# A transformer layer in fp32 with 16 experts on one Trainium2 core: attention and projection joined in one stage, row-maxima pieces, list matmuls and last loads in another order

## The reference

```python
def _L0_attn_ref(x, W_qkv, W_proj):          # 2048 tokens, D = 512, 16 heads of 32
    qkv = x @ W_qkv.T
    attn = jnp.einsum('bhqd,bhkd->bhqk', q, k) * SCALE
    attn = jnp.where(causal[None, None], attn, -jnp.inf)
    out = jnp.einsum('bhqk,bhkd->bhqd', jax.nn.softmax(attn, axis=-1), v)
    return out.transpose(0, 2, 1, 3).reshape(b, s, d) @ W_proj.T
def _moe_forward(x, gate_w, w_gate, w_up, w_down):       # E = 16, K = 6
    scores = jax.nn.softmax(h @ gate_w.T, axis=-1)
    topk_w, topk_idx = jax.lax.top_k(scores, K)
    cw = jnp.zeros((T, E)).at[jnp.arange(T)[:, None], topk_idx].add(topk_w)
    for e in range(E):
        y = y + cw[:, e:e + 1] * (silu(h @ w_gate[e].T) * (h @ w_up[e].T) @ w_down[e].T)
x = x + _layernorm(_L0_attn_ref(_layernorm(x), L0_attn_W_qkv, L0_attn_W_proj))
x = x + _layernorm(_L0_ffn_ref(_layernorm(x), gate_w, w_gate, w_up, w_down))
```

## Time and profile before

| | |
|---|---|
| median of 3 runs | 1742.45 us (1741.38 to 1743.12) |
| the profiled execution | 1742.76 us, of which the span of the trace is 1740.9 us |
| busy, share of the span | PE 96%, DVE 67%, ACT 64%, POOL 55% |
| mean granted clock of PE | 0.98 |
| start and embedding | 0 to 168 us |
| attention | 168 to 822 us |
| projection, router, lists | 822 to 942 us |
| experts | to 1702 us |
| end | to 1740.9 us |

### The profile page before, as it was taken

The page is one execution under the profiler, slowest core; times in us unless marked ns, Lnnn a source line. Parts: engine busy times, 40 slices in busy tenths (PEclk is TensorE's granted clock), DMA queues, the critical chain, the costliest instruction groups (busy, mean ns, idle before and its releaser), DMA issues.

```text
span 1740.9 us, 30524 instructions
## 1 busy us (share of the span) xinstructions
PE 1665.3 (96%) x9254; PEld 1372.2 (79%) x9254; DVE 1167.9 (67%) x2371; ACT 1105.5 (64%) x1684; POOL 954.5 (55%) x836
## 2 busy tenths in 40 slices
PE   7999999999999999998995999999999999999995
PEld 7987767676777777764764999999999999999992
DVE  6437777777777777777687666665665565556555
ACT  3222887778787887776575665665665565556544
POOL 2321888888888888886663343434343434343423
PEclk9999999999999999999995999999999999999997
DMA  8676111111111111220662887987887787788766
GB/s 247 189 218 194 49 50 49 49 49 49 49 49 49 49 49 49 59 63 28 222 249 87 295 266 205 281 243 224 264 248 195 229 255 217 217 247 235 190 196 212
DMA packets 103700, 276.88 MB, mean 159 GB/s; under 512 B 19817, under 2 KB 37609, under 8 KB 93609
## 3 DMA queue, kind: packets, MB, share of 16 engines
q1 hardware_dynamic: 78153, 213.29, 37.3%
q0 software_dynamic: 25440, 62.27, 16.7%
HBM read 194.75 MB, written 63.72 MB: 148 GB/s over the span
## 4 chain that ended last, share of the span: by engine, by line
PE 44%; DVE 4%; DMA 2%; issue 1%; ACT 1%; POOL 1%; SPq 0%; DVEq 0%; POOLq 0%; ACTq 0%
PE p_prj L91 25%; PE p_logit_ps L91 6%; PE p_at_ps L91 6%; PE p_ht_ps L2045 3%; PE p_at_ps L2068 2%; DMA h_rows<-p_hn 1%; DVE r_lane_hot L1749 1%; DVE rows L1917 1%; DMA acc_rows<-m_y_out,m_row_ids 1%; DVE p_st L1755 0%; PE p_list_ps L1998 0%; DMA m_w_raw<-acc_rows 0%; PE p_logit_ps L1956 0%; DVE m_w_lo L1878 0%; POOL p_rstd L1414 0%
## 5 line engine op out<-in xcount | busy, mean ns | idle before, releaser
L709 POOL TENSOR_TENSOR prob_lo<-prob,prob_hi 128x1024 fp32r<-128x1024 f32 x217 | 465.5, 2166 | 127.0 <-DVE prob_hi L787 125.2
L759 DVE TENSOR_REDUCE part_max<-a_mp 128x1 f32<-128x512 f32 (+2 forms) x600 | 358.9, 610 | 70.9 <-PE a_mp L841 41.5
L1452 POOL DMA_INDIRECT acc_rows<-m_y_out,m_row_ids x108 | 175.9, 1629 | 412.3 <-ACT m_y_out L1618 391.9
L744 ACT ACTIVATE prob<-a_sp 128x1024 f32<-128x1024 f32 x320 | 293.7, 930 | 67.0 <-PE a_sp L904 36.8
L91 PE MATMUL p_prj<-m_w_hi,m_ht_hi 128*128 128x352 f32 x888 | 297.5, 335 | 1.6 <-DVE m_ht_lo L1854 1.5
L91 PE MATMUL p_prj<-m_w_lo,m_ht_hi 128*128 128x352 f32 x888 | 288.3, 325 | 0.0
L91 PE MATMUL p_prj<-m_w_hi,m_ht_lo 128*128 128x352 f32 x888 | 287.7, 324 | 0.0
L1878 DVE TENSOR_TENSOR m_w_lo<-m_w_raw,m_w_hi 128x704 fp32r<-128x704 f32 (+1 forms) x357 | 270.6, 797 | 22.9 <-ACT m_w_hi L1624 22.5
L1624 ACT ACTIVATE m_w_hi<-m_w_raw 128x704 fp32r<-128x704 f32 (+1 forms) x357 | 229.0, 713 | 17.8 <-PE p_prj L91 16.9
L1864 DVE TENSOR_TENSOR m_at_lo<-p_at_ps,m_at_hi 128x384 fp32r<-128x384 f32 x111 | 61.8, 557 | 252.2 <-ACT m_at_hi L1610 252.2
L731 ACT ACTIVATE prob_hi<-prob 128x1024 fp32r<-128x1024 f32 x216 | 203.3, 941 | 6.9
(11 more groups left out here) (309 smaller groups left out, 3378.6 us busy)
## 6 DMA issues: line engine op xcount, KB each, us to landing
m_w_raw<-wexp SPq DMA_DIRECT2D x51, 1408.0 KB, 6.9
m_w_raw<-wexp SPq DMA_DIRECT2D x51, 768.0 KB, 5.5
qk_parts<-rows SPq DMA_DIRECT2D x64, 256.0 KB, 3.2
multi<-qk_parts SPq DMA_DIRECT2D x42, 256.0 KB, 4.7
acc_rows<-p_zeros SPq DMA_DIRECT2D x2, 4352.0 KB, 18.8
v_head<-v_all SPq DMA_DIRECT2D x16, 520.0 KB, 3.0
k_stack<-qk_parts SPq DMA_DIRECT2D x21, 256.0 KB, 4.1
q_stack<-qk_parts SPq DMA_DIRECT2D x21, 256.0 KB, 5.9
```

Source lines behind the costliest of these rows:

```text
L709: nc.gpsimd.tensor_tensor(prob_lo[:, t % RING, :, c0:NB], prob[:, t % RING, :, c0:NB], f32(prob_hi[:, t % RING, :, c0:NB]), ALU.subtract). ...
L744: nc.scalar.activation(prob[:, t % RING, :, c0:NB], sp_[:, t % 2, :, c0:NB], ACT.Exp, scale=SCALE).then_inc(prob_ready, 1)
L759: nc.vector.reduce_max(part_max[:, qb, kb:kb + 1], mp[:, n % 2, 0:width], AX_X).then_inc(piece_done, 1)
L1452: nc.gpsimd.indirect_dma_start(acc_dram[sum_of(t)], bass.IndirectOffsetOnAxis(ap=row_id(t), axis=0), y_out[:, t % 4, :], None, compute_op= ...
```

## The change

It has seven parts, told here in the order of the program.

Part A, the start: SP issues the second quarter of the rows when the first has landed; ACT splits the first half of the value weights ahead of the turned rows, and DVE likewise.

Part B, the pieces of head 0 beside the units: 40 pieces over 10 units in place of 11. PE turns the second half's maxima inside the unit that follows the last piece, and DVE evicts them behind the pieces of that unit.

Part C: `PIECES_AT_FIRST` has three pieces fewer in the first three steps, and three more between steps 7 and 19.

Part D: attention and projection stand in one block. PE turns the first tile of attention before the last four steps of `times_v` are complete, runs the first projection right behind them, and makes the last `turn_out` after it. ACT, DVE and POOL do their first projection work ahead of the last `copy_out`, `read_out` and `store_out`. SP loads `x_in` at the first value step of the last head, and the first expert's weights at its last. The first set of expert weight buffers lies elsewhere in SBUF.

Part E: near the end of the router, `list_tokens` of tiles 6 to 9 each stand one step later among `turn_normal` and `router_logits`.

Part F: the last lists are made in the order 11, 12, 14, 13, 15, and the last one waits for its edges one by one.

Part G, the end: tiles 12 and 13 are summed on PE and no longer on POOL. The first four loads are single tiles (before, the first two), six pairs follow, and each load from the fourth on waits for the landing of the one three before it. POOL adds tiles 14 and 15 right after the power of the first group.

```diff
-HEAD0_UNITS = 11
+HEAD0_UNITS = 10
@@ embedding, SP
         for s in range(4):
+            if s == 1:
+                sp.wait_ge(x_landed[0], 16)
             sp.dma_start(x_in[:, s, :], x_dram[s]).then_inc(x_landed[s], 16)
@@ embedding, ACT
-        act.wait_ge(tp_ready, 1)
-        nc.scalar.activation(xt_hi[:, 0], tp[:, 0], ACT.Copy).then_inc(xt_hi_done, 1)
         for v in range(VPIECES):
             act.wait_ge(wv_landed[v], 16)
             nc.scalar.activation(w_hi[v], w_raw[...], ACT.Copy).then_inc(wv_hi_done, 1)
+            if v == 0:
+                act.wait_ge(tp_ready, 1)
+                nc.scalar.activation(xt_hi[:, 0], tp[:, 0], ACT.Copy).then_inc(xt_hi_done, 1)
@@ embedding, DVE
         normalise(0, 0)
+        value_weights_low(0)
         turned_low(0, 0)
-        value_weights_low(0)
@@ embedding, DVE, unit n
-            for part in head0_turned_at(n):
-                maxima_out(part)
             for i in head0_pieces(n):
                 piece(i)
...
+            for part in head0_turned_at(n):
+                maxima_out(part)
@@ embedding, PE, unit n, after piece c of four
-            for part in head0_turned_at(n):
-                turn_maxima(part)
+                if c == 1:
+                    for part in head0_turned_at(n - 1):
+                        turn_maxima(part)
@@
-PIECES_AT_FIRST = (2, 2, 2, 2, 2, 3, 3, 2, 2, 2, 1, 2, 1, 2, 2, 2, 2, 2, 2, 2)
+PIECES_AT_FIRST = (1, 1, 1, 2, 2, 3, 3, 3, 3, 2, 1, 2, 1, 2, 2, 2, 2, 2, 3, 2)
@@ attention, POOL, ACT, DVE: the last output is returned, to be called later
-        store_out(H - 1, H * NTB - 1, NTB - 1)
+        return lambda: store_out(H - 1, H * NTB - 1, NTB - 1)
-        copy_out(H * NTB - 1, NTB - 1, H * NS)
+        return lambda: copy_out(H * NTB - 1, NTB - 1, H * NS)
-        read_out(H * NTB - 1)
+        return lambda: read_out(H * NTB - 1)
@@ attention, PE
-        for t in range(NS - LAG, NS):
-            times_v(H - 1, (H - 1) % 2, t)
-        pe.wait_ge(out_read, H * NTB - 1)
-        turn_out(H * NTB - 1, NTB - 1)
+        times_v(H - 1, (H - 1) % 2, NS - LAG, (0,))
+        def last_values():
+            times_v(H - 1, (H - 1) % 2, NS - LAG, (1,))
+            for t in range(NS - LAG + 1, NS):
+                times_v(H - 1, (H - 1) % 2, t)
+        def last_turn():
+            pe.wait_ge(out_read, H * NTB - 1)
+            turn_out(H * NTB - 1, NTB - 1)
@@ the end
-POOL_SUMS = (0, 2, 12, 13, 14, 15)
+POOL_SUMS = (0, 2, 14, 15)
-LAST_LOADS = ((0, 1), (1, 2)) + tuple((t, t + 2) for t in range(2, NT, 2))
+LAST_LOADS = ((0, 1), (1, 2), (2, 3), (3, 4)) + tuple((t, t + 2) for t in range(4, NT, 2))
@@ joined block, SP
+            sp.wait_ge(pv_done, (H - 1) * NS + 1)
             for s in range(4):
                 sp.dma_start(x_in[:, s, :], x_dram[s]).then_inc(x_landed[s], 16)
+            sp.wait_ge(pv_done, H * NS)
             sp.dma_start(w_raw[0][:], w_dram[0]).then_inc(wexp_landed, 16)
...
             for q, (lo, hi) in enumerate(LAST_LOADS):
+                if q >= 3:
+                    sp.wait_ge(acc_summed[q - 3], 16)
@@ joined block, POOL
+            pool.wait_ge(pv_done, H * NS)
             nc.gpsimd.memset(zeros[:], 0.0).then_inc(zeros_set, 1)
...
             constants()
+            last_output()
...
-                if q < 2:
-                    add_loaded(12 + 2 * q)
-                    add_loaded(13 + 2 * q)
+                if q == 0:
+                    add_loaded(14)
+                    add_loaded(15)
@@ joined block, DVE, tile t
                     attention_low(t + 1)
+                if t == 0:
+                    last_output()
@@ joined block, PE
             turn_attention(0)
+            last_values()
...
                 project(t)
+                if t == 0:
+                    last_turn()
...
             router_logits(NT - 3)
+            turn_normal(NT - 2)
             list_tokens(6)
-            turn_normal(NT - 2)
-            list_tokens(7)
             router_logits(NT - 2)
             turn_normal(NT - 1)
+            list_tokens(7)
+            router_logits(NT - 1)
             list_tokens(8)
-            router_logits(NT - 1)
+            turn_logits(3)
             list_tokens(9)
-            turn_logits(3)
             list_tokens(10)
...
-            for s in range(11, NT):
+            for s in (11, 12, 14, 13, 15):
                 list_tokens(s)
```

61 lines of the change are left out of this document (29 added, 32 removed).

## The result

The changed kernel takes 1727.02 us (median of 4 runs, 1723.85 to 1728.81), the kernel before 1742.78 (1741.38 to 1745.75): ratio 0.9904, 95% interval 0.9887 to 0.9921. A second, later set gave 1725.25 against 1743.84, ratio 0.9893 (0.9876 to 0.9909). The forecast was 1725.7, range 1720 to 1732. The profiled execution took 1726.77, its span is 1725.0.

The account below looks back on a forecast made before the run. PE was taken as busy almost throughout attention and experts, so gains come only at edges and add up: 0.8 + 2.2 + 0.5 + 7.1 + 3.7 + 1.0 + 1.5 = 16.8; 1742.76 - 16.8 - 0.3 = 1725.7 us, range 1720 to 1732.

Parts of the forecast that it names:

- I take 0.8, nearer the upper end: Start: earlier split of the value weights gains 0.8 us from a range of 0 to 1.2, since DVE works in order.
- Both waits: Head 0: PE's waits of 0.99 and 1.28 us for the row maxima would go, 2.27 together.
- The wait of 0.72: Head 0's first steps: PE waits 0.72 us at 173.61 for the row maximum of an earlier piece.
- with one piece a step it should go: Head 0's first steps: fewer pieces would remove PE's 0.72 us wait for a row maximum; 0.5 us taken.
- if the turn of tile 1 overlaps wholly: Seam of attention and projection: upper case, 7.7 us gained in place of 7.1.
- I take the waits themselves: Router's end: moving lists one step later gains PE's waits for list inputs, 3.7 us, from a range of 1.8 to 4.7.
- The check from POOL's side: End: for DVE's second group to start 1.5 us earlier, the last load must land by 1721.8; called close.
- rival 2: End: idle queues and POOL's wait for the last load eat the gain there; 1727.2 to 1728.7 us, chance 0.11.
- the prediction's other sum, of 18.0: Whole kernel: by the shared-port rule, removing a pair of POOL sums is worth 3.2, not 2.0; time 1724.4 us.
- Rival 3: Attention: the 3.5 us PE is earlier in head 0 are taken back by POOL or transfers; 1729.2 us, chance 0.06.
- Rivals 1 and 4: Projections: PE at half clock in the first only, 1728.1 us, chance 0.15; or through the projections, slower, 1760, chance 0.03.
- rival 5: Head 0 and router waits return one step later, seam gives its lower end; 1731.5 us, chance 0.08.

Follow-up runs that it names:

- undo_c: Changed kernel with the old `PIECES_AT_FIRST` list; first scores of head 0 to ACT's last copy measured 654.37 us.
- undo_e: Changed kernel with the router's lists in their old order; branch of tile 15 to the maximum of the last logits measured 12.89 us.
- d_alone: Kernel before plus only the joined attention and projection block, and the last list waiting for edges one by one; 1734.81 us, ratio 0.9954.
- gap: Changed kernel with the last attention turn ahead of the first projection and PE waiting there for POOL's constants; last copy to first branch 11.11 us.
- turn_first: Changed kernel with the last attention turn made ahead of the first projection; last copy to first branch 6.41 us.

## Why the prediction was right

The sum was 16.8 us; the trace gives 15.9 (DVE's last step 1737.55 to 1721.64), the medians 15.8 and 18.6. The frame was right: the gains came at the edges where PE waits, and added up. By its steps:

- **A, 0.8 forecast, -0.4 measured** (70.56 before, 70.9 in the mean of nine traces). The order of the splits gave what it should, 0.6 where the clock rises at the same time. The step that failed is "I take 0.8, nearer the upper end": the sum had no term for PE's clock, which is at the lower level at the start and rose 2 to 4 us later in six of the nine traces. The mechanism named against the 0.8, that the second half of the weights is issued later, did come in part of the traces (up to 1.6 us later), and DVE, which waited for it, took its next step at 13.04 and not before 12.62. The range's lower end of 0 was too high.
- **B, 2.2 forecast, 3.0 measured.** Both waits went, 2.3 together, as forecast; the other 0.7 was not foreseen, and stays open. A wait for DVE came, as the prediction feared, but behind the edge (0.8, for `rows`).
- **C, 0.5 forecast.** Against the kernel before, the stretch is no shorter (650.8 in the mean for 649.9, 651.6, 649.8). At the fourth copy of ACT, past the first head's differences, the changed kernel stands at 45.84 and the kernel before at 45.67. The wait of 0.72 went and 3.1 us of waits for DVE and a load are in its place, at a full clock where it had been 0.79. The step that failed is that "with one piece a step it should go" was priced as if no other wait took its place. undo_c shows what the list is for: without it, and with part B, PE loses 1.2 us there, and 0.9 more at a slower clock.
- **D, 7.1 forecast, 7.7 to 8.2 measured.** The upper end that the text gave (7.7, "if the turn of tile 1 overlaps wholly") was the case: the projection began 0.16 after the copy. The clock was at the full level, as the forecast's likeliest case had it; POOL's constants delayed the branch by 0.08 at most (2.48 us from the statistics, 2.40 before).
- **E, 3.7 forecast, 4.6 between the two kernels.** The step that failed is "I take the waits themselves": undo_e leaves 2.4 for the order of lists, since part of the waits was refilled by others (for `p_hn`, 2.4 before, 3.0 now). The other 2.2 is the clock, which comes back sooner in the joined stage with no change to the work; this was not in the forecast, and is luck.
- **F, 1.0 forecast, 0.95 measured.** One list of three went, as worked out. No run undoes it alone; d_alone and the kernel before have 17.63, all with the new order 16.7 to 16.8.
- **G, 1.5 forecast, 1.2 in the mean** (30.8 in three traces to 29.6 in eight). Its gains were larger than taken: tile 3 came 0.9 sooner in the given trace (0.7 forecast), and the whole 2.0 of the sums beside DVE's first group went (0.8 forecast). The check from POOL's side, that the last load must land by 14.4 us after the first issue, was the right one: it landed at 16.07, and DVE's wait of 2.15 for the power took most of that back. This is the mechanism of rival 2, in part. So the size was right by two errors that balanced. In the prediction's other sum, of 18.0, two things are off: it adds 1.2 for the sums where only 0.8 of the 2.0 had been taken, and the 3.21 is itself drawn out by the overlap, since two sums alone take 2.5 (1.27 each).
- **Between the edges**: the experts took 751.5 for 751.0 and 749.9, and 749.4 to 751.5 over all traces, as "no matmul is taken out" said. Rival 3 did not come as a loss of B; A and C gave nothing by themselves. Rivals 1 and 4 did not come. Of rival 5, neither the waits of B nor those of E came back in full.

That the sum came so close is in part luck: A, C, the order of E and G were too high by 1.2, some 0.5, 1.3 and 0.3, and this was balanced by B and D, too low by 0.8 and 0.6 to 1.1, and by the 2.2 of the clock in the router, which the sum did not have.

## What to carry to other kernels

Where a kernel's middle stretches have PE busy all the time, cut its trace at the edges, at the same instruction in both kernels: the stretches then tell parts apart that the total can't (at the edges of B, D and F traces of one kernel agree to 0.1 to 0.5 us, their totals only to 4 or 5). Edges that hang on loads (G) or on the clock (A, E, the last quarter of attention) spread by 1.3 to 2.6, and there one trace says little unless its clock is laid beside it. A long wait at a stage's seam can cost twice, once itself and once by the slower clock behind it (gap: 3.1 and 1.5 us), and work put into the seam saves both; a short one (0.33 in turn_first) costs itself alone. A load that is held back to help another must be priced by what waits for the held one: of the two such waits here, neither is shown to have given anything.
